# Mamba block between two feed-forward halves, one core: depthwise convolution of two of four channel blocks on TensorE, output projection added by VectorE from its bank, and a segment's side work placed anew

## Chip, cores and metric

One core of a Trainium2 chip. The metric is the device time of one launch in microseconds, the median over several runs. The launch gets all inputs in HBM and writes one output there.

## The reference, cut to what matters

The input has 4 sequences of 1024 tokens with 256 channels, float32 throughout. Three sublayers follow one another: a gated feed-forward part (three cycles of a small coupling network), a selective state-space (Mamba) block, and the feed-forward part again. The change lies in the middle one:

```
xn   = rmsnorm(layernorm(x)) * norm_w             # 256 channels
skip = xn @ skip_w.T ;  x = xn @ in_w.T           # 512 channels
xc[t] = conv_b + sum_k x[t-3+k] * conv_w[:, k]    # depthwise, 4 taps
x    = silu(xc)
delta = softplus((x @ wd1.T) @ wd2.T + wd2_b) ;  B, C = x @ wB.T, x @ wC.T
h[t] = exp(delta[t] * A) * h[t-1] + (delta[t] * x[t]) * B[t]    # 512 x 16 states
y[t] = sum_n h[t, :, n] * C[t, n] + W_D * x[t]
out  = (y * silu(skip)) @ out_w.T ;  result = resid + out
```

## The kernel before, in words

`build` (L1459) runs three programs behind one another, with all engines meeting in between: `ffn` on the input, `mamba`, and `ffn` again with the output stored. Only `mamba` (L719), the last lines of `kernel` and nothing of the feed-forward parts are touched.

**Segments and units.** `mamba` cuts the tokens into 8 segments of 512 (two halves of each sequence). The 512 channels are 4 blocks of 128 partitions (c = 0 to 3). A segment i is 32 units: for each pair of blocks (q = 0, 1) and each of the 16 states n, one unit. K counts units over all segments. Each engine has its own program that walks over K; semaphores with counts tie them. In one unit:

- GpSimd (`drive`, L1155) multiplies dx by the broadcast row of B into u, 128x1024. It may be four units ahead (U_RING).
- ScalarE (`decay`, L957) writes exp(delta * A) of both blocks into one of two PSUM tiles a_bank. It may refill one when the unit two before is done with it. In even segments it also copies the last column of each scan to `carry` (L969), which the odd segments start from.
- VectorE (`scan`, L1285) runs the recurrence along the 512 tokens of both blocks, one operand in PSUM. In 20 of 32 units it also multiplies by the row of C (`weigh`, L1297). In the 12 others (POOL_N: 0, 2, 5, 7, 10, 12 of each 16) the scan goes to SBUF and GpSimd weighs it (L1167), three units later.
- TensorE (`add_up`, L1442) adds the weighed states into y_bank by a product with the identity. At units 2 and 18 `feed_through` (L1430) starts a new sum with the D term, after `finish` (L1307, VectorE, units 1 and 17) has taken the last one and multiplied it by the gate.
- SyncE loads the rows of B and C, two units to a transfer, into rings of three.

**Side work.** Beside the recurrence of segment i, segment i + 1 is prepared (p = i + 1): input projection ("in", L1405), convolution, SiLU (L1027), projection to delta's rank, B and C ("xproj", L1410, copied by L1035 and stored to DRAM by SyncE at row pair 9), step size ("dt", L1414, copied by L1040), softplus (L1047), dx = delta * x on GpSimd (L1176). The skip projection of segment i itself gives the gate (tanh on ScalarE, L1112; `gate_skip` on VectorE, L1347), the output projection of segment i - 1 ("out", L1419) is copied by ScalarE (`take_out`, L1117) and added to x_tok by GpSimd (`out_add`, L1184), and the tokens of segment i + 2 are normalised (L979) and turned ("turn", L1399; L1001).

Two tables written by hand set the order: `PLACES` gives the units at which TensorE does each piece, `AT` the units at which the other engines do theirs. An engine does its side work of a unit behind that unit's recurrence. All TensorE side work goes through two banks, w_bank, in turn; `released` says whose signal frees a use for the next but one. Segment 0 is prepared ahead of the recurrence, in the a_banks.

**Convolution.** ScalarE's `accumulate` (L1019) starts an accumulator (it shares dx's storage) with the last tap and the bias. `convolve` (L1337) on VectorE adds the three other taps from the bank, shifted by one to three tokens, three scalar_tensor_tensor in place, each waiting for the one before. Since the second half of a sequence needs the last three tokens of the first, `keep_spill` (L1314, L1319, L1323) computes their part in three small operations per block when a first half is prepared, and `accumulate` puts it in by three single-column operations (L1017).

**Norms.** `norms(1, 0)` and `norms(1, 1)`, at units 5 and 10 of segment 0, compute the scales of the later tokens in operations of 128x16 (L1216 to L1230).

Of the kernel before, what the change touches and what calls it, by code (L numbers as in the profile page):

```python
# [718 lines left out]
def mamba(nc, mem, bc_rows):  # L719
# [21 lines left out]

    PLACES = {
        "in": ((0, 0), (1, 1), (3, 3), (4, 4)),
        "out": ((6, 6), (7, 7)),
        "xproj": ((10, 10),),
        "skip": ((11, 11), (14, 14), (19, 19), (20, 20)),
        "dt": ((13,), (15,), (16,), (17,)),
        "turn": ((24,), (25,)),
# [19 lines left out]
        "dx": (23, 24),  # L768
        "out_add": (13, 14),
# [27 lines left out]
    def exists(i, kind):  # L797
        return {"out": puts_out(i), "skip": core(i), "turn": turns(i)}.get(kind, prep(i))
# [22 lines left out]

    def released(use):

        i, kind, c = use
        p = i + 1
        if use[:2] == (-1, "in"):
            return "spill", c + 1
        return {"turn": ("xn", 2 * p + c + 3), "out": ("out_there", 2 * (i - 1) + c + 1), "in": ("conv", KE * p + c + 1),
                "xproj": ("proj", p + 1), "dt": ("step", KE * p + c + 1), "skip": ("gated", KE * i + c + 1)}[kind]

    with ExitStack() as ctx:
# [34 lines left out]
        one_col = sb("one_col", [P, 1])  # L866

# [8 lines left out]
            "xn_tok", "xn", "z", "work_done", "acc", "taps", "spill_part", "spill", "conv", "x",  # L876
            "proj", "bc_stored", "tanh_s", "gated", "step", "delta", "dx0", "dx1",
            "brow0", "brow1", "brow2", "crow0", "crow1", "crow2",
            "u", "a", "scan", "carry", "hc", "hc_pool", "y_dve", "y_pool", "y", "out_there", "out_added")}
# [16 lines left out]
        def _(sp):  # L896
            for i in range(-1, SEGS):
                for r in range(PASS):
# [17 lines left out]
                    if prep(i) and r == 9:  # L916
# [4 lines left out]
        def _(act):  # L921
# [83 lines left out]
            def accumulate(i, c):  # L1005
# [4 lines left out]
                if c == 0 and i > 0:  # L1010
                    act.wait_ge(S["u"], i * UNITS)
                lo = 0
                if ph == 1:
                    lo = TAPS - 1
                    act.wait_ge(S["spill"], p // 2 * KE + c + 1)
# [7 lines left out]
            def silu(i, c):  # L1023

                p = i + 1
                act.wait_ge(S["conv"], p * KE + c + 1)
# [494 lines left out]
```

## Time and profile before

| | us |
|---|---|
| median of 3 runs (lowest to highest) | 1326.85 (1325.11 to 1328.06) |
| the profiled execution, its own time | 1325.21 |
| its span in the trace | 1323.4 |
| VectorE busy | 1184.1 (89%) |
| TensorE busy | 1061.0 (80%) |
| GpSimd busy | 872.6 (66%) |
| ScalarE busy | 774.8 (59%) |
| recurrence of `mamba` (first scan to last weighing) | 224.8 to 1131 |

Busy is the share of the span in which an engine has an instruction under way. Matmuls are pipelined and their ends modelled, so TensorE's share is not its share at peak; a float32 product stands as two instructions. Rows of the timeline merge neighbouring instructions of one kind; within a row they overlap a little, so the distance between starts is what one costs. "[x <-E]" is idle time of the engine ahead of the instruction and what ended it. DVE is VectorE, ACT ScalarE, POOL GpSimd, PE TensorE.

### The profile page before, as it was taken

The page shows a single profiled execution, that of the slowest core. Times are in us where ns is not written, and L with a number is a line of the kernel's source. Part 1 is how long each engine was busy: PE and PEld are TensorE (multiplying, and loading weights), DVE is VectorE, ACT ScalarE, POOL GpSimd, SP SyncE. Part 2 cuts the span into 40 slices and gives each one's busy share as a digit, 9 for nine tenths or more (in the row PEclk, how much of TensorE's full clock was granted, in tenths as well). Part 3 has the DMA queues.
Part 4 walks back from the last instruction along what each step waited for, and adds up shares of the span by engine and source line. Part 5 has one row for each costly group of instructions (what it writes and reads, how often), then busy time and mean ns, then how long its engine had stood idle before and what let it go on. Part 6 is the DMA issues. An engine that isn't in the chain of part 4 may idle for free. (4 is left out here: it accounts for less than half of the span.)

```text
span 1323.4 us, 10922 instructions
## 1 busy us (share of the span) xinstructions
PE 1061.0 (80%) x2688; PEld 456.6 (35%) x2688; DVE 1184.1 (89%) x1768; ACT 774.8 (59%) x1321; POOL 872.6 (66%) x390
## 2 busy tenths in 40 slices
PE   3999746687889788888878988987897867799973
PEld 2434212233343343334334333432432422444421
DVE  3765898999999999999999999999999999576587
ACT  2656658757456566745666664665674434265665
POOL 0000004889989999998999999899999999000000
PEclk9999978799999999999989989999998889899998
DMA  6000003244543535343444444445444443000003
GB/s 207 1 1 1 1 1 113 96 160 133 170 141 130 181 112 185 127 159 128 149 169 141 165 142 149 140 126 191 139 149 162 137 177 112 0 1 1 1 1 128
DMA packets 48000, 146.56 MB, mean 111 GB/s; under 512 B 5504, under 2 KB 14336, under 8 KB 47936
## 3 DMA queue, kind: packets, MB, share of 16 engines
q1 hardware_dynamic: 47440, 145.03, 33.1%
q10 hardware_dynamic: 496, 0.82, 0.2%
q8 instruction: 22, 0.36, 0.1%
q14 instruction: 42, 0.34, 0.1%
HBM read 141.05 MB, written 4.72 MB: 110 GB/s over the span
## 5 line engine op out<-in xcount | busy, mean ns | idle before, releaser
L1155 POOL TENSOR_TENSOR late<-m_dx,m_brow 128x1024 f32<-128x1024 f32 x256 | 597.7, 2363 | 6.7 <-DVE m_a_bank L1285 6.5
L957 ACT ACTIVATE m_a_bank<-m_delta,m_negA 128x512 f32<-128x512 f32 x512 | 335.1, 683 | 174.6 <-DVE m_hc L1297 134.0
L1442 PE MATMUL m_y_bank<-m_hc,ident 128*128 128x512 f32 x640 | 332.4, 645 | 116.1 <-DVE m_hc L1297 115.4
L1167 POOL TENSOR_TENSOR m_hc_pool<-m_hid,m_crow 128x1024 f32<-128x1024 f32 x96 | 226.8, 2363 | 31.0 <-DVE m_hid L1285 30.6
L1442 PEld LDWEIGHTS m_y_bank<-m_hc,ident 128*128 128x128 f32 x640 | 119.6, 201 | 305.1 <-DVE m_hc L1297 186.7
L1297 DVE TENSOR_TENSOR m_hc<-m_a_bank,m_crow 128x512 f32<-128x512 f32 x320 | 203.0, 677 | 0.0
L1285 DVE TENSOR_TENSOR_SCAN m_a_bank<-m_a_bank,m_carry,late 128x512 f32<-128x512 f32 x160 | 196.4, 1274 | 1.1 <-ACT m_a_bank L957 0.8
L1285 DVE TENSOR_TENSOR_SCAN m_a_bank<-m_a_bank,late 128x512 f32<-128x512 f32 x160 | 186.7, 1212 | 7.0 <-ACT m_a_bank L957 3.7
L1442 PE MATMUL m_y_bank<-m_hc_pool,ident 128*128 128x512 f32 x384 | 188.0, 613 | 4.9 <-POOL m_hc_pool L1167 4.9
L1176 POOL TENSOR_TENSOR m_dx<-m_delta,m_x 128x1024 f32<-128x1024 f32 x16 | 38.0, 2377 | 216.5 <-ACT m_delta L1047 216.5
L1285 DVE TENSOR_TENSOR_SCAN m_hid<-m_a_bank,m_carry,late 128x512 f32<-128x512 f32 x96 | 117.7, 1269 | 0.0
L1405 PE MATMUL m_w_bank<-m_xn,w 128*128 128x512 f32 x240 | 112.5, 596 | 2.5 <-DVE m_dx L1337 2.4
L1285 DVE TENSOR_TENSOR_SCAN m_hid<-m_a_bank,late 128x512 f32<-128x512 f32 x96 | 111.8, 1206 | 1.4 <-ACT m_a_bank L957 1.4
L1442 PEld LDWEIGHTS m_y_bank<-m_hc_pool,ident 128*128 128x128 f32 x384 | 75.7, 199 | 104.1 <-issue 88.6
L432 PE MATMUL f_pair<-f_h,w 128*128 128x512 f32 x192 | 92.5, 609 | 8.4 <-ACT f_h L549 8.4
L969 ACT ACTIVATE m_carry<-m_a_bank 128x2 f32<-128x2 f32 x80 | 13.5, 169 | 111.1 <-DVE m_hc L1297 111.1
L1430 PE MATMUL m_y_bank<-m_x,m_diag_d 128*128 128x512 f32 x64 | 41.2, 778 | 33.8 <-DVE m_gate L1307 33.8
L1419 PE MATMUL m_w_bank<-w,m_gate 128*128 128x256 f32 x256 | 59.1, 384 | 9.6 <-DVE m_dx L1337 8.1
L1405 PEld LDWEIGHTS m_w_bank<-m_xn,w 128*128 128x128 f32 x240 | 44.9, 190 | 62.9 <-issue 53.8
L481 PE MATMUL f_pair<-f_z,w 128*128 128x512 f32 x128 | 65.4, 592 | 0.0
L549 ACT ACTIVATE f_h<-f_a,w 128x512 f32<-128x512 f32 x96 | 63.6, 712 | 1.0 <-DVE f_a L271 1.0
L1337 DVE SCALAR_TENSOR_TENSOR m_dx<-m_w_bank,m_conv,m_dx 128x511 f32<-128x511 f32 (+2 forms) x84 | 62.2, 741 | 1.1
(148 smaller groups left out, 1237.9 us busy)
## 6 DMA issues: line engine op xcount, KB each, us to landing
m_brow<-bc_rows SPq DMA_DIRECT2D x128, 512.0 KB, 5.0
m_crow<-bc_rows SPq DMA_DIRECT2D x128, 512.0 KB, 4.1
x_tok<-x_in SPq DMA_DIRECT2D x4, 1024.0 KB, 8.6
out<-x_tok SPq DMA_DIRECT2D x3, 1024.0 KB, 4.8
w<-w_in SPq DMA_DIRECT2D x1, 1024.0 KB, 11.6
out<-x_tok SPq DMA_DIRECT2D x4, 256.0 KB, 2.1
w<-w_in SPq DMA_DIRECT2D x1, 750.0 KB, 10.4
w<-w_in ACTq DMA_DIRECT2D x1, 512.0 KB, 6.0
```

The costliest lines, as they stand in the source:

```text
L432: last = nc.tensor.matmul(pair[2][:, h, :], w(w256, W256, "w2", k), h1[:, k, half(h)], start=k == 0, stop=k == KD - 1)
L481: last = nc.tensor.matmul(out[:, m, :], second, z[:, b % 2, 1, half(n)], start=False, stop=True)
L549: nc.scalar.activation(h1[:, m, half(h)], source, ACT.Gelu, bias=w128[:, o:o + 1]).then_inc(h1_ready, 1)
L957: nc.scalar.activation(a_bank[K % 2][:, j, :], delta[:, i % 2, c, :], ACT.Exp, scale=negA[:, c, n:n + 1]).then_inc(S["a"], 1)
L1155: nc.gpsimd.tensor_tensor(u[:, K % U_RING, :, :], dx[:, i % 2, 2 * q:2 * q + 2, :], brow[:, K // 2 % ROW_RING, K % 2, :].unsqueeze(1).to_b ...
L1167: nc.gpsimd.tensor_tensor(hc_pool[:, before % POOL_RING, :, :], hid[:, before % POOL_RING, :, :], crow[:, K // 2 % ROW_RING, K % 2, :].uns ...
L1285: nc.vector.tensor_tensor_scan(hid[:, pool_before(K) % POOL_RING, j, :] if by_pool(K) else a, a, u[:, K % U_RING, j, :], 0.0 if i % 2 == 0 ...
L1297: nc.vector.tensor_tensor(hc[:, before % HC_RING, j, :], a_bank[K % 2][:, j, :], crow[:, K // 2 % ROW_RING, K % 2, :], ALU.mult).then_inc( ...
L1337: nc.vector.scalar_tensor_tensor(a[:, s:], b[:, 0:BANK - s], conv[:, c, k:k + 1], a[:, s:], ALU.mult, ALU.add)\
L1405: op = nc.tensor.matmul(b, w256[:, part, o:o + P], xn[:, (p if kind == "in" else i) % 2, part, :], start=part == 0, stop=part == KD - 1)
L1419: op = nc.tensor.matmul(b[:, part * DIM:(part + 1) * DIM], gate[:, d, at:at + P], col("out", d, DIM), start=d == 0, stop=d == KE - 1)
L1442: op = nc.tensor.matmul(y_bank[:, j, :], ident[:, :], source[:, before % ring, j, :], start=False, stop=K % PASS == PASS - 1)
```

## The change

Blocks 2 and 3 (PE_CONV) are convolved by TensorE in all segments but segment 0's preparation: ScalarE copies the projection to `raw` in SBUF behind its last three tokens, TensorE multiplies four shifted windows of it by four diagonal matrices (`diag_w`) and sums them in a bank ("taps"), and the SiLU reads that bank with the bias. No spill is kept for these blocks. Blocks 0 and 1 stay as they were. VectorE adds the output projection straight from its bank; ScalarE's copy and GpSimd's add are gone. The two tables are new. The four tensor_tensor of `norms` (L1218, L1220, L1227, L1230) become scalar_tensor_tensor with a factor 1. The final statistics are taken inside VectorE's loop, which is longer. The scratch for descriptors is given as 8192.

```diff
+    PE_CONV = (2, 3)
     PLACES = {
         "in": ((0, 0), (1, 1), (3, 3), (4, 4)),
         "out": ((6, 6), (7, 7)),
-        "xproj": ((10, 10),),
-        "skip": ((11, 11), (14, 14), (19, 19), (20, 20)),
-        "dt": ((13,), (15,), (16,), (17,)),
-        "turn": ((24,), (25,)),
+        "skip": ((9, 9), (10, 10), (24, 24), (25, 25)),
+        "taps": ((), (), (12, 12, 13, 13), (13, 13, 14, 14)),
+        "xproj": ((18, 18),),
+        "dt": ((20,), (21,), (22,), (23,)),
+        "turn": ((27,), (28,)),
     }
     AT = {
         "acc": (2, 3, 5, 6),
-        "silu": (8, 8, 8, 8),
-        "out_there": (9, 10),
-        "proj": (12,),
-        "tanh_s": (13, 16, 21, 22),
-        "step": (15, 17, 18, 19),
-        "softplus": (20,),
-        "xn_tok": (23, 24),
-        "xn": (26, 27),
-        "z": (28, 29),
-        "conv": (2, 3, 5, 6),
-        "gate": (13, 16, 21, 22),
+        "tanh_s": (11, 12, 26, 27),
+        "silu": (17, 17, 17, 17),
+        "proj": (20,),
+        "step": (22, 23, 24, 25),
+        "softplus": (25,),
+        "xn_tok": (25, 26),
+        "xn": (29, 30),
+        "z": (30, 31),
+        "conv": (2, 3),
+        "out_add": (8, 9),
+        "gate": (11, 12, 26, 27),
         "finish": (1, 17),
-        "dx": (23, 24),
-        "out_add": (13, 14),
+        "dx": (28, 29),
     }
...
+        if kind == "in" and p > 0 and c in PE_CONV:
+            return "raw", 2 * p + c - 1
...
+        raw = sb("raw", [P, 2, TAPS - 1 + BANK])
+        diag_w = sb("diag_w", [P, 2, TAPS, P])
...
-                    if prep(i) and r == 9:
+                    if prep(i) and r == (13 if i >= 0 else 9):
                         sp.wait_ge(S["proj"], i + 2)
...
+                if c in PE_CONV and p > 0:
+
+                    if ph == 0:
+                        act.wait_ge(S["none"], 1)
+                    nc.scalar.activation(raw[:, c - 2, 0:TAPS - 1], none[:, :] if ph == 0 else raw[:, c - 2, BANK:],
+                                         ACT.Copy).then_inc(S["history"], 1)
+                    act.wait_ge(S["history"], 2 * (p - 1) + c - 1)
+                    nc.scalar.activation(raw[:, c - 2, TAPS - 1:], b, ACT.Copy).then_inc(S["raw"], 1)
+                    return
+                if c in PE_CONV:
+                    nc.scalar.activation(raw[:, c - 2, BANK:], b[:, BANK - TAPS + 1:], ACT.Copy).then_inc(S["raw"], 1)
...
-                act.wait_ge(S["conv"], p * KE + c + 1)
+                if c in PE_CONV and p > 0:
+                    nc.scalar.activation(x[:, p % 2, c, :], work_there((i, "taps", c)), ACT.Silu,
+                                         bias=conv[:, c, TAPS:TAPS + 1]).then_inc(S["x"], 1)
+                    return
+                act.wait_ge(S["conv"], conv_count(p, c))
...
-                if c == 0:
-                    act.wait_ge(S["out_added"], 2 * i)
-                if c >= 2:
+                if i > 0 or c >= 2:
                     act.wait_ge(S["gated"], i * KE + c - 1)
...
-                    nc.vector.tensor_tensor(square, rstd[:, ts], rstd[:, ts], ALU.mult).then_inc(S["square"], 1)
+                    nc.vector.scalar_tensor_tensor(square, rstd[:, ts], 1.0, rstd[:, ts], ALU.mult, ALU.mult)\
+                        .then_inc(S["square"], 1)
...
+            nc.vector.memset(none[:, :], 0.0).then_inc(S["none"], 1)
+            for c in PE_CONV:
+                for s in range(TAPS):
+                    op = nc.vector.tensor_scalar(diag_w[:, c - 2, s, :], ident[:, :], w512[:, c, o + s:o + s + 1], None,
+                                                 ALU.mult)
+            op.then_inc(S["diag_w"], 1)
...
+            def out_add(i, c):
+
+                dve.wait_ge(S["work_done"], USES.index((i, "out", c)) + 1)
+                dve.wait_ge(S["z"], 2 * i)
+                at = (i - 1) * HT + 2 * c
+                to = x_tok[:, at:at + 2, :].rearrange("p a d -> p (a d)")
+                nc.vector.tensor_tensor(to, to, bank_of((i, "out", c)), ALU.add).then_inc(S["out_added"], 1)
...
-            for K in range(-UNITS, TOTAL + 2):
+            for K in range(-UNITS, TOTAL + UNITS):
...
+                if K == TOTAL + 2:
+                    final_measure()
+                for c in due(k, "out_add") if puts_out(i) else ():
+                    out_add(i, c)
...
                 if K == AT["conv"][-1] - UNITS:
-                    for c in range(KE):
+                    for c in PE_CONV:
+                        convolve(i, c)
+                    for c in range(KE - len(PE_CONV)):
                         keep_spill(-1, c, 1)
                         keep_spill(-1, c, 2)
...
+                elif kind == "taps":
+                    if part == 0:
+                        pe.wait_ge(S["diag_w"], 1)
+                        pe.wait_ge(S["raw"], 2 * p + c - 1)
+                    op = nc.tensor.matmul(b, diag_w[:, c - 2, part, :], raw[:, c - 2, part:part + BANK],
+                                          start=part == 0, stop=part == TAPS - 1)
...
-    nc = bacc.Bacc("TRN2", target_bir_lowering=False, num_devices=1)
+    nc = bacc.Bacc("TRN2", target_bir_lowering=False, num_devices=1, dynamic_dma_scratch_size=8192)
```

## Rows read from the trace of the kernel before

**Rows 1.** Busy time by stretch: segments 0, 1, 2; columns named in the first row.
```profile
core 0: us, PE busy (x) PEld busy (x) DVE busy (x) ACT busy (x) POOL busy (x), PEclk, DMA share, GB/s
224.80:344.40 119.60, 87.31 (x176) 34.39 (x176) 117.52 (x131) 79.17 (x153) 107.15 (x48) 0.87 0.42 135
344.40:459.00 114.60, 95.28 (x225) 41.15 (x224) 114.19 (x138) 66.28 (x103) 109.42 (x50) 0.97 0.46 148
459.00:570.70 111.70, 96.07 (x225) 41.62 (x224) 109.15 (x125) 72.73 (x144) 108.51 (x49) 0.95 0.43 151
```
**Rows 2.** Groups of instructions, VectorE, segment 2; busy, mean ns, idle before, releasers.
```profile
L1285 DVE TENSOR_TENSOR_SCAN m_a_bank<-m_a_bank,late 128x512 f32<-128x512 f32 x40 | 46.7, 1212 | 1.9 <-POOL late L1155 1.0 <-ACT m_a_bank L957 0.9
```
**Rows 3.** Timeline, GpSimd, segment 0; start, length, instruction.
```profile
241.40 7.00 POOL L1155 TENSOR_TENSOR late<-m_dx,m_brow 128x1024 f32<-128x1024 f32 x3
```
**Rows 4.** Timeline, VectorE, a convolution in segments 2 (even) and 1 (odd).
```profile
470.30 2.34 DVE L1285 TENSOR_TENSOR_SCAN m_a_bank<-m_a_bank,late 128x512 f32<-128x512 f32 x2
472.55 1.27 DVE L1297 TENSOR_TENSOR m_hc<-m_a_bank,m_crow 128x512 f32<-128x512 f32 x2
473.73 2.31 DVE L1337 SCALAR_TENSOR_TENSOR m_dx<-m_w_bank,m_conv,m_dx 128x511 f32<-128x511 f32 x3
...
353.91 0.73 DVE L1337 SCALAR_TENSOR_TENSOR m_dx<-m_w_bank,m_conv,m_dx 128x511 f32<-128x511 f32 x1
356.44 2.46 DVE L1285 TENSOR_TENSOR_SCAN m_a_bank<-m_a_bank,m_carry,late 128x512 f32<-128x512 f32 x2
```
**Rows 5.** Waits of segment 7 (first row), then timeline of the tail.
```profile
DVE m_gate L1347 <- ACT m_th L1112: 2.9, 1, 2.9
...
1141.57 0.60 ACT L1117 ACTIVATE m_th<-m_w_bank 128x512 f32<-128x512 f32 x1 [2.86 <-PE m_w_bank L1419]
1142.24 1.26 POOL L1184 TENSOR_TENSOR x_tok<-x_tok,m_th 128x512 f32<-128x512 f32 x1 [2.19 <-ACT m_th L1117]
```
**Rows 6.** TensorE, segments 2 and 3: projection, restarts behind finish; then one stretch's clock.
```profile
502.26 3.60 PE L1410 MATMUL m_w_bank<-m_x,w 128*96 128x512 f32 x8
...
525.92 3.26 PE L1430 MATMUL m_y_bank<-m_x,m_diag_d 128*128 128x512 f32 x4 [1.92 <-DVE m_gate L1307]
...
531.15 1.88 PE L1442 MATMUL m_y_bank<-m_hc_pool,ident 128*128 128x512 f32 x4
...
640.50 1.98 PE L1430 MATMUL m_y_bank<-m_x,m_diag_d 128*128 128x512 f32 x4 [2.29 <-DVE m_gate L1307]
...
526.00:530.00 4.00, 4.00 (x6) 1.70 (x7) 4.00 (x4) 2.62 (x6) 4.00 (x3) 0.57 0.65 260
```
**Rows 7.** Timeline, ScalarE, around the four SiLUs of segment 2.
```profile
488.97 1.28 ACT L1027 ACT_TABLE_LOAD   x1
...
493.92 1.30 ACT L957 ACTIVATE m_a_bank<-m_delta,m_negA 128x512 f32<-128x512 f32 x2
```
**Rows 8.** Timeline around the softplus, segments 2 (first three) and 3.
```profile
526.21 0.67 ACT L1040 ACTIVATE m_delta<-m_w_bank,w 128x512 f32<-128x512 f32 x1
...
535.30 2.34 DVE L1285 TENSOR_TENSOR_SCAN m_hid<-m_a_bank,late 128x512 f32<-128x512 f32 x2 [0.35 <-ACT m_a_bank L957]
...
540.24 1.08 ACT L979 ACTIVATE m_tmp_u<-x_tok,m_shift_n,m_scale_n 128x256 f32<-128x256 f32 x2
...
648.17 1.30 ACT L957 ACTIVATE m_a_bank<-m_delta,m_negA 128x512 f32<-128x512 f32 x2
649.81 2.46 DVE L1285 TENSOR_TENSOR_SCAN m_hid<-m_a_bank,m_carry,late 128x512 f32<-128x512 f32 x2
```
**Rows 9.** Timeline, VectorE, norms in segment 0.
```profile
248.68 4.35 DVE L1218 TENSOR_TENSOR m_roots<-m_rstd 128x16 f32<-128x16 f32 x1
...
271.59 2.28 DVE L1225 SCALAR_TENSOR_TENSOR m_shift<-moments,m_rstd 128x16 f32<-128x16 f32 x1
```
**Rows 10.** Timeline, VectorE, prologue ahead of the first scan.
```profile
202.32 0.75 DVE L1337 SCALAR_TENSOR_TENSOR m_dx<-m_a_bank,m_conv,m_dx 128x511 f32<-128x511 f32 x1 [2.77 <-ACT m_dx L1019]
...
213.32 0.27 DVE L1314 TENSOR_SCALAR m_spill<-m_a_bank,m_conv 128x3 f32<-128x3 f32 x1
...
214.02 0.34 DVE L1248 SCALAR_TENSOR_TENSOR x_tok<-late,coef,x_tok 128x128 f32<-128x128 f32 x1
```

More of the change, by code:

```diff
@@ L797, in exists @@
     def exists(i, kind):
-        return {"out": puts_out(i), "skip": core(i), "turn": turns(i)}.get(kind, prep(i))
+        return {"out": puts_out(i), "skip": core(i), "turn": turns(i), "taps": prep(i) and i >= 0}.get(kind, prep(i))
     def bank_name(i, kind, c, index):
@@ L825, in released @@
         p = i + 1
-        if use[:2] == (-1, "in"):
+        if kind == "in" and p == 0 and c not in PE_CONV:
             return "spill", c + 1
-        return {"turn": ("xn", 2 * p + c + 3), "out": ("out_there", 2 * (i - 1) + c + 1), "in": ("conv", KE * p + c + 1),
+        if kind == "in" and p > 0 and c in PE_CONV:
+            return "raw", 2 * p + c - 1
+        return {"turn": ("xn", 2 * p + c + 3), "out": ("out_added", 2 * (i - 1) + c + 1), "in": ("conv", conv_count(p, c)),
+                "taps": ("x", KE * p + c + 1),
                 "xproj": ("proj", p + 1), "dt": ("step", KE * p + c + 1), "skip": ("gated", KE * i + c + 1)}[kind]
@@ L875, in mamba @@
             "negA", "expA", "late_by_dve", "late_straight", "late_added", "late_stats", "moments", "root", "square", "rstd", "diag_d", "final_stats", "constants",
-            "xn_tok", "xn", "z", "work_done", "acc", "taps", "spill_part", "spill", "conv", "x",
+            "xn_tok", "xn", "z", "work_done", "acc", "history", "raw", "none", "diag_w", "taps", "spill_part", "spill", "conv", "x",
             "proj", "bc_stored", "tanh_s", "gated", "step", "delta", "dx0", "dx1",
             "brow0", "brow1", "brow2", "crow0", "crow1", "crow2",
-            "u", "a", "scan", "carry", "hc", "hc_pool", "y_dve", "y_pool", "y", "out_there", "out_added")}
+            "u", "a", "scan", "carry", "hc", "hc_pool", "y_dve", "y_pool", "y", "out_added")}
         block = ctx.enter_context(nc.Block())
@@ L1014, in accumulate @@
                     lo = TAPS - 1
-                    act.wait_ge(S["spill"], p // 2 * KE + c + 1)
+                    act.wait_ge(S["spill"], p // 2 * 2 + c + 1)
                     for j in range(lo):
@@ L1341, in convolve, with final_measure @@
                         keep_spill(i, c, s)
+            def out_add(i, c):
[4 more added lines that the diff above has]
+                nc.vector.tensor_tensor(to, to, bank_of((i, "out", c)), ALU.add).then_inc(S["out_added"], 1)
+            def final_measure():
+                dve.wait_ge(S["out_added"], 2 * 2 * HALVES)
+                for t in range(2 * BT):
+                    op = nc.vector.bn_stats(final_stats[:, t, :], x_tok[:, t, :])
+                op.then_inc(S["final_stats"], 1)
+                dve.wait_ge(S["final_stats"], 1)
+                for t in range(2 * BT):
+                    nc.vector.bn_aggr(moments[:, t, :], final_stats[:, t, :])
             def gate_skip(i, c):
-                if c == 0 and puts_out(i):
-                    dve.wait_ge(S["out_there"], 2 * i)
                 dve.wait_ge(S["tanh_s"], i * KE + c + 1)
```

40 lines of the change are left out of this document (12 added, 28 removed).

## The prediction

> **What bounds the kernel now.** I cut the span into its parts with the table of busy time by stretch [rows 1]: the recurrence runs from 224.8 to 1131 us, 68% of the span, as eight segments of 32 units. Apart from the prologue ahead of it and the hand-over behind it, all the work that the change touches lies there. VectorE (DVE) is busy 109.15 of the 111.70 us of segment 2 and 114.19 of the 114.60 of segment 1, so it sets the pace. Odd segments start from carries and keep the convolution's spill, and are longer. The groups of instructions give what little DVE waits: in segment 2, 1.0 us for POOL and 0.9 for ScalarE (ACT) before scans [rows 2], the rest in gaps of 0.3 to 0.4. GpSimd (POOL) is close behind: three products in a row take 7.00 us, one every 2.32 [rows 3]. A segment has 32 products for u, 12 weighings and 2 for dx, 46 x 2.32 = 106.7 us, and POOL's two output adds on top (108.5 to 109.4 busy). So DVE work that goes is worth its full time only down to some 107 us a segment, and only if what is moved makes no new wait. TensorE (PE) has 96 of 112 us busy, with modelled ends.
>
> **The change, part by part.**
>
> *Convolution.* On DVE the three operations of a block stand with 2.31 us in an even segment, 2.25 of it their own (neighbours overlap, as the scan pair of 2.34 shows, behind which the next starts after 2.25); with the spill in an odd segment it is 2.53, 353.91 to 356.44 [rows 4]. Two blocks go from each of seven segments: 4.5 or 5.1 us.
>
> *Output adds.* DVE gets two adds of 128x512 with one operand in PSUM. The nearest row has the same engine, operation and kinds of operand: two in 1.18 us (472.55 to 473.73), 0.59 each [rows 4]. I take 1.2 us a segment (segments 1 to 7); bounds 1.1 and, at the price of a convolution's operation, 2.31 / 3, 1.5. POOL loses 2.5 us, ACT two copies of 0.60 [rows 5].
>
> *PE.* Eight products for the taps. The four products (8 instructions) of the projection take 3.6 us [rows 6], so 7 us a segment, bounded by 14 at half clock. PE is not the bound on average, 96 + 7 of 109; where it could be is a rival below.
>
> *ACT on blocks 2 and 3.* Copies replace scaled copies of like size, and three single-column operations each go in even segments; the SiLU reads a bank instead of an accumulator. I price it at nothing: units 2 to 6 of these segments are where DVE convolves and ACT is ahead. Bounds minus 0.5 and plus 0.5.
>
> *SiLUs at unit 17.* At unit 8 today the table load starts at 488.97 and the next decay only at 493.92 [rows 7]: 5 us, which two scans and a weighing on DVE just cover. At 17 the next unit is a POOL one (no weighing on DVE, 1.2 us less cover), set off by finish (1.2 us more), but the decay of 17 is itself released later by a carry: counting the rows through from the start of scan 16, the decay of 18 is ready at 7.45 us and DVE at 2.25 + 3.43 + 1.19 = 6.87. Late by 0.6 in even segments; without the carry copies and with longer scans, nothing in odd ones.
>
> *Projection at 18 and 20.* It now stands behind finish(17) and PE's feed-through. Today PE goes from the feed-through to its third group in 5.23 us in segment 2 (525.92 to 531.15); in segment 3, where the feed-through takes 1.98 and not 3.26, it is some 3.5 [rows 6]. With 3.6 for the projection, 0.6 for ACT's copy and 0.95 for the carry and half a decay, scan 21's input stands 17.4 us after scan 16's start at the slow rate, 15.8 at the fast; DVE wants it at 16.6. Late by 0 to 0.9; 0.5 in even segments, 0 in odd ones.
>
> *Softplus at 25, beside step(3) and the first xn_tok.* Units 24, 25, 26 have the pattern of 19, 20, 21. Today scan 21 waits 0.35 us [rows 8]. Two things are added ahead of the next decay: the step of 0.67, done a unit earlier today, and the xn_tok pair of 1.08. So 0.35 + 0.67 + 1.08 = 2.1 us late at scan 26 in even segments. In odd ones that decay has 0.9 us in hand (its first half is over at 648.86, the scan starts at 649.81 [rows 8]), so 0.85. One more xn_tok and a tanh at 26 put scan 27 0.25 late in even ones.
>
> *Sum of new waits:* 0.6 + 0.5 + 2.1 + 0.25 = 3.45 us in an even segment, 0.9 to 1.0 in an odd one. They replace 2.55 and 0.4.
>
> *POOL.* Its dx products move to 28 and 29. It gets to u(28) only when scan 24 has ended, and the softplus is over before scan 25 ends, so it loses at most the time of one product; a wait for scan 26 ahead of weighing 26 comes to it, from its lead. With 106.7 us of work in segments of 109 to 111.5 it keeps a lead, and the 1.0 us DVE waits for it goes.
>
> *SP.* The store of B and C moves from row pair 9 to 13, behind the row loads that wait for unit 21, so the projection (by then copied) never holds the queue. One issue stands ahead of the next row load either way: nothing.
>
> *Norms* (four tensor_tensor become scalar_tensor_tensor). In segment 0 the tensor_tensor of 128x16 takes 4.35 us and the scalar_tensor_tensor of 128x16 takes 2.28 [rows 9], for 16 elements a partition. Both forms wait, so I give the edit 0; its bounds are minus 4.2 and plus 2.3.
> The Trainium skill says of this (SBUF — State Buffer, on the shared port pair) that VectorE and GpSimd lock one pair of ports for a whole instruction, and that a VectorE instruction with two SBUF inputs needs it; by that rule, with which the trace agrees, the new form gains nothing, and by a rule that tied the stall to tensor_tensor the sum would be 4.2 lower. It also speaks for the new output add, one of whose inputs is in PSUM.
>
> *Prologue.* The spill of two blocks goes from DVE's unbroken run to the first scan: 0.70 each (213.32 to 214.02), minus 1.4 [rows 10]. The eight scaled identities of 128x128, at most the 0.34 us of the 128x128 operation at 214.02, are 2.7 us in the 2.77 that DVE idles ahead of the first convolution [rows 10]: nothing; uncovered they would cost 2.7.
>
> *Last segment and tail.* DVE's wait of 2.9 us for the gate, held up by the output copies and POOL's adds, goes [rows 5]; 1.2 of adds come and a POOL wait of 0.3 goes: minus 2.0, of which I take 1.7. After the recurrence ACT's copy (0.60) and POOL's add (1.26) give way to one DVE add of 0.68 [rows 5]: minus 1.2. The loop's longer range and the move of the final statistics cost nothing: they run while PE multiplies.
>
> *Sum.* Prologue -1.4. Segment 0: -4.5, old waits of 2.1 (119.60 less 117.52) for new ones of 3.45, -3.1. Segments 2, 4, 6: -4.5 + 1.2 - 2.55 + 3.45 = -2.4 each, -7.2. Segments 1, 3, 5: -5.1 + 1.2 - 0.4 + 1.0 = -3.3 each, -9.9. Last segment -1.7, tail -1.2. In all -24.5 us. The profiled execution took 1325.21 us (span 1323.4), which gives 1300.7; the median of the runs shown, 1326.85, stands 1.6 higher, so 1302.3.
>
> **Rivals.**
>
> *The new waits don't come; POOL is the limit.* For it: DVE's own work is then 105.8 (even) and 110.4 (odd), and half a unit of ACT's lead would swallow the 0.6 and 0.5. Against it: today's 0.35 us at the softplus shows ACT with no reserve there. Even segments would fall to 106.7 (-5.0), odd ones by 4.3, segment 0 by 6.6: -1.4 - 6.6 - 15 - 12.9 - 3.2 = -39, 1288.
>
> *The clock at PE's restart.* In segment 2 the groups behind finish run mostly at the lower of the two levels, 1.2 GHz (granted clock 0.57 from 526 to 530), after PE has idled 1.92 us [rows 6]. If the projection too runs there it takes 7.2 in place of 3.6, and finish, feed-through, projection, copy and decay become one chain through four engines: 3.6 later, of which DVE feels some 2 to 3.4 in each of seven segments. Against it: odd segments restart at 2.4 GHz, and PE idles less with the taps. -24 + 7 x 2 = -10, 1316; at worst 1326.
>
> *PE becomes the bound ahead of finish (slower).* From the end of unit 4 to finish(17) PE has 13 sums of 1.72 (half the projection's eight instructions, less their overlap), the outputs' 6.9, two skips and the taps, 3.4 + 6.9: 39.6 us. DVE reaches finish(17) after 41.1 in an even segment (five POOL units of 2.25, eight of its own at 2.25 + 1.18, two adds and two gates at 0.6), 42.4 in an odd. A microsecond at 1.2 GHz costs half a microsecond; with over 10 us of it in that stretch in each of seven segments, DVE would wait 3.5 us at each finish and all the gain would be gone. At 15 us it waits some 5.5: +39 - 24, 1342. Against it: PE has no gap there after which the clock fell.
>
> *It doesn't do what it says:* DVE's busy time falls, but the old waits, moved, take all of it: 1327.
>
> **Numbers.** Forecast with its neighbourhood (1293 to 1309) 0.58; POOL limit 0.12; restart chain 0.19, a few hundredths of it within 0.2%; PE bound 0.06; no gain 0.05. Range 1291 to 1316: most of the POOL case and the restart case at 2 us a segment. A measurement here can tell 0.2% (2.7 us) from no change. Faster 0.87, same 0.06, slower 0.07.
>
> **What would show it.** DVE's STT on convolution banks down from 12 to 6 a segment; busy 105.9 (even) and 110.4 (odd); segments of 109.3 and 111.4; a wait of about 2 us for ACT at scan 26 (0.9 odd), under 1 at 18 and 21; POOL without idle cost to DVE; norms' stalls still 2 to 4 us; first scan at 223.4. Wrong if waits at finish(17) exceed 1 us (PE), if scan 21 waits over 2 us (restart), or if scan 26 starts on time (POOL limit).

## The result, and the profile after

The changed kernel takes 1316.5 us, the median of 4 runs (1315.76 to 1318.55), against 1326.42 of 4 runs of the kernel before: a ratio of 0.9927, with a 95% interval of 0.991 to 0.9944. It is faster, as forecast, but by 9.9 us and not by 24.5. The profiled execution took 1316.35 us with a span of 1314.6 (before: 1325.21 and 1323.4). Of the twelve executions of e5 below, one took 1823.45 us at a granted clock of 0.557 and is left out of what is said of e5.

First the busy time by engine, from the page of the changed kernel, and then its table of busy time by stretch for segments 1, 2, 5 and 6 (columns as in [rows 1]).

```profile
PE 1090.7 (83%) x2800; PEld 479.5 (36%) x2800; DVE 1162.0 (88%) x1727; ACT 760.6 (58%) x1298; POOL 853.1 (65%) x374
```
```profile
341.80:456.40 114.60, 98.85 (x242) 43.91 (x240) 110.50 (x127) 64.93 (x103) 107.25 (x47) 0.99 0.44 147
456.40:568.00 111.60, 100.35 (x241) 44.56 (x240) 106.11 (x121) 70.18 (x138) 106.05 (x47) 0.97 0.47 151
...
794.00:909.80 115.80, 101.58 (x241) 44.98 (x240) 110.53 (x128) 65.08 (x103) 107.24 (x47) 0.96 0.43 146
909.80:1018.60 108.80, 97.51 (x233) 43.20 (x232) 105.89 (x122) 64.73 (x126) 104.31 (x46) 0.98 0.46 153
```

Beside [rows 1] the reader is to see that VectorE's work fell as worked out: 114.19 to 110.50 in segment 1 (110.4 was forecast), 109.15 to 106.11 in segment 2 (105.9 was forecast). But segments 1 and 2 are as long as before, 114.6 and 111.6. The eight segments' lengths, from first scan to first scan and to the last weighing for segment 7, are 117.9, 114.6, 111.6, 114.4, 111.6, 115.8, 108.8 and 105.1 us; before, 119.7, 114.6, 111.7, 114.6, 111.8, 114.6, 111.7 and 107.4. The forecast had 21.9 us less in them, and 6.3 came. Segments 1, 3 and 5 fall short by 3.3, 3.1 and 4.5, segments 2 and 4 by 2.3 and 2.2, segment 0 by 1.3; segments 6 and 7 beat it by about half a microsecond each.

The work that went was replaced by waits. The groups of instructions on VectorE in segment 2 (as [rows 2]):

```profile
L1303 DVE TENSOR_TENSOR_SCAN m_a_bank<-m_a_bank,late 128x512 f32<-128x512 f32 x40 | 46.6, 1212 | 1.2 <-ACT m_a_bank L970 1.2
L1303 DVE TENSOR_TENSOR_SCAN m_hid<-m_a_bank,late 128x512 f32<-128x512 f32 x24 | 28.0, 1208 | 4.1 <-ACT m_a_bank L970 4.1
...
L1355 DVE SCALAR_TENSOR_TENSOR m_dx<-m_w_bank,m_conv,m_dx 128x511 f32<-128x511 f32 (+2 forms) x6 | 4.5, 743 | 0.1
...
L1367 DVE TENSOR_TENSOR x_tok<-x_tok,m_w_bank 128x512 f32<-128x512 f32 x2 | 1.4, 680 | 0.0
```

The six operations of convolution and the two new adds stand there as planned, and the wait for GpSimd is gone. In its place are 5.3 us of waits for ScalarE's decay; before, it was 1.3 us for ScalarE and 1.0 for GpSimd. By unit, the waits before scans are: in segments 2 and 4, 0.64 at scan 18, 0.66 at 21, 1.24 at 24, 2.8 at 26; in segments 1 and 3, 0.77 and 0.59 at 21, 0.91 at 24, 2.35 at 26; in segment 5, 1.93 at 21 and the rest alike. Segment 6 has no wait at 21, 0.3 at 24 and 1.82 at 26. The forecast had 0.6, 0.5, nothing and 2.1 in an even segment, and 0.85 at scan 26 alone in an odd one. So scan 18 is right, scan 24 was not foreseen, scan 26 is 0.7 over in even segments and 1.5 in odd ones, and the 0.25 forecast at scan 27 did not come.

What ScalarE waited for stands in the table of waits over the recurrence (total us, number of waits, longest):

```profile
ACT m_proj L1063 <- PE m_w_bank L1448: 32.9, 7, 7.0
...
ACT m_delta L1068 <- PE m_w_bank L1452: 25.9, 15, 2.8
...
DVE m_hid L1303 <- ACT m_a_bank L970: 23.9, 15, 2.8
```

ScalarE waits for the projection (seven times, once for each segment that is prepared) and then for the products of the step size. The chain in segment 3, first TensorE's timeline, then ScalarE's, then VectorE's (scans 21, 24 and 26):

```profile
633.51 3.50 PE L1468 MATMUL m_y_bank<-m_x,m_diag_d 128*128 128x512 f32 x4 [3.85 <-DVE m_gate L1325]
636.84 1.88 PE L1480 MATMUL m_y_bank<-m_hc,ident 128*128 128x512 f32 x4
638.56 3.60 PE L1448 MATMUL m_w_bank<-m_x,w 128*96 128x512 f32 x8
...
645.52 1.12 PE L1452 MATMUL m_w_bank<-m_proj,w 64*128 64x512 f32 x2
...
654.03 1.12 PE L1452 MATMUL m_w_bank<-m_proj,w 64*128 64x512 f32 x2
```
```profile
642.19 0.59 ACT L1063 ACTIVATE m_proj<-m_w_bank 96x512 f32<-96x512 f32 x1 [5.64 <-PE m_w_bank L1448]
...
651.36 0.69 ACT L1068 ACTIVATE m_delta<-m_w_bank,w 128x512 f32<-128x512 f32 x1 [2.80 <-PE m_w_bank L1452]
...
655.19 0.69 ACT L1068 ACTIVATE m_delta<-m_w_bank,w 128x512 f32<-128x512 f32 x1 [0.15 <-PE m_w_bank L1452]
655.89 1.28 ACT L1075 ACT_TABLE_LOAD   x1
```
```profile
643.50 2.46 DVE L1303 TENSOR_TENSOR_SCAN m_hid<-m_a_bank,m_carry,late 128x512 f32<-128x512 f32 x2 [0.59 <-ACT m_a_bank L970]
...
652.76 2.47 DVE L1303 TENSOR_TENSOR_SCAN m_a_bank<-m_a_bank,m_carry,late 128x512 f32<-128x512 f32 x2 [0.91 <-ACT m_a_bank L970]
...
662.31 2.46 DVE L1303 TENSOR_TENSOR_SCAN m_hid<-m_a_bank,m_carry,late 128x512 f32<-128x512 f32 x2 [2.35 <-ACT m_a_bank L970]
```

TensorE stands for 3.85 us at the feed-through until finish(17) is done, and only then does the projection behind it, though its last input was there at 630.7 (the end of the SiLUs). From 633.51 to the last product of the step size at 654.03 it has no idle row. Each product comes late, ScalarE stands before the step of each (2.80 at the worst, and with it the decay for scan 24), and the last step, still held by TensorE (0.15), puts the start of the softplus, the table load at 655.89, 3.1 us after the start of scan 24. Scan 26 pays for it.

The recorded expectations below weigh two theories. **Theory A**: TensorE is late, because it idles for finish, restarts at the lower level of its clock, and only then does the projection. **Theory B**: ScalarE has more work between units 17 and 27 than fits, whoever feeds it. Theory A has two halves, which e7 and e8 part. *The place*: the projection is queued behind the wait for finish. *The clock*: what is queued there restarts at the lower level.

### The profile page after: what moved, and what is told of

Read it like the earlier page. It is cut to its first block and busy times, and to the rows that moved or that the text cites. A ratio compares the mean times of both kernels' runs of the same rounds, so it can differ in the third digit from the quotient of the medians.

```text
span 1314.6 us, 11061 instructions
## 1 busy us (share of the span) xinstructions
PE 1090.7 (83%) x2800; PEld 479.5 (36%) x2800; DVE 1162.0 (88%) x1727; ACT 760.6 (58%) x1298; POOL 853.1 (65%) x374
## 5 line engine op out<-in xcount | busy, mean ns | idle before, releaser
L1480 PE MATMUL m_y_bank<-m_hc,ident 128*128 128x512 f32 x640 | 326.1, 634 | 85.8 <-DVE m_hc L1315 85.8
L1480 PE MATMUL m_y_bank<-m_hc_pool,ident 128*128 128x512 f32 x384 | 183.6, 601 | 0.0
L1303 DVE TENSOR_TENSOR_SCAN m_hid<-m_a_bank,late 128x512 f32<-128x512 f32 x96 | 111.8, 1206 | 13.6 <-ACT m_a_bank L970 13.5
L256 DVE TENSOR_SCALAR f_cpl<-f_cpl,f_slope,f_base 128x512 f32<-128x512 f32 x32 | 17.4, 543 | 42.2 <-ACT f_cpl L581 42.1
```

The source lines that it names most:

```text
L1303: nc.vector.tensor_tensor_scan(hid[:, pool_before(K) % POOL_RING, j, :] if by_pool(K) else a, a, u[:, K % U_RING, j, :], 0.0 if i % 2 == 0 ...
L1480: op = nc.tensor.matmul(y_bank[:, j, :], ident[:, :], source[:, before % ring, j, :], start=False, stop=K % PASS == PASS - 1)
```

## The experiments

Each was run beside the kernel before, on the same chip as it: 1327.5 us (7 runs) for the first four, 1327.39 (17 runs) on another chip for the others. Each edit is against the changed kernel, where nothing else is said, and "..." marks lines left out. A caution for small differences of totals: the feed-forward part behind `mamba`, which no edit touches, takes 179.3 us in the profiled executions of the changed kernel and of e8 (granted clock 0.956), 179.9 in the kernel before, and 180.8 to 181.5 in the others (0.94). So the readings below go by segment.

**The projection one unit earlier, ahead of finish (e1).**

```diff
-        "xproj": ((18, 18),),
+        "xproj": ((17, 17),),
```

> The changed kernel with one number changed: the projection to rank, B and C at TensorE's unit 17 in place of 18, so that it stands ahead of the feed-through that waits for finish(17), and no longer behind it. Theory A (TensorE gets late: it idles 2.4 to 3.9 us for finish(17), restarts at the low clock, and only then does the projection, so that scans 21 and 24 and in part 26 wait for ScalarE, which waits for TensorE): the waits at scan 21 (0.6 to 1.9 us) and 24 (0.9 to 1.2) go, scan 26 waits 0.9 (odd) or 2.1 (even) in place of 2.35 and 2.8; sum over the segments some 15 us, 1301 us. Theory B (ScalarE itself has more work between units 17 and 27 than fits, whoever feeds it): the waits only change places, 1316 us. A third outcome, the feed-through late by 1.5 us making sums and finish late: slower than 1316.

Measured: 1297.68 us (1297.12 to 1298.28), ratio 0.9776 (0.9761 to 0.979). One unit in a table takes 19 us off. Its busy time by stretch for segments 1 and 2, and its timelines of TensorE and of ScalarE in segment 3:

```profile
340.70:451.90 111.20, 99.25 (x241) 44.02 (x240) 110.33 (x128) 65.34 (x103) 106.65 (x47) 0.98 0.45 151
451.90:560.50 108.60, 99.01 (x241) 44.10 (x240) 105.87 (x121) 70.42 (x138) 106.42 (x47) 0.98 0.45 155
```
```profile
622.56 3.67 PE L1448 MATMUL m_w_bank<-m_x,w 128*96 128x512 f32 x8 [0.53 <-ACT m_x L1051]
626.07 1.88 PE L1468 MATMUL m_y_bank<-m_x,m_diag_d 128*128 128x512 f32 x4
...
631.78 1.98 PE L1480 MATMUL m_y_bank<-m_hc,ident 128*128 128x512 f32 x4 [0.40 <-DVE m_hc L1315]
...
635.33 1.98 PE L1480 MATMUL m_y_bank<-m_hc,ident 128*128 128x512 f32 x4 [0.51 <-DVE m_hc L1315]
```
```profile
644.30 0.69 ACT L1068 ACTIVATE m_delta<-m_w_bank,w 128x512 f32<-128x512 f32 x1
645.01 1.28 ACT L1075 ACT_TABLE_LOAD   x1
```

The 3.67 us of the projection now lie in the time in which TensorE stood for finish. It comes to the feed-through without a gap and at full speed (four instructions in 1.88), and soon waits for VectorE again (0.40, 0.51): it has caught up. The last step does not wait for TensorE, and the softplus starts 1.55 us after scan 24 (643.46 to 645.01), not 3.1. VectorE's waits in this run are 0.64 at scan 18 and 1.95 at scan 26 in even segments, 0.8 at scan 26 in odd ones, and none at 21 or 24. These are the forecast's own 0.6, 2.1 and 0.85, and the segments of 111.2 and 108.6 stand beside its 111.4 and 109.3. Theory B is out: the waits at 21 and 24 went, they did not change places. Both halves of theory A allow this, since the idle stretch and the place went together: the seven restarts behind finish(17) in segments 0 to 6 are all at the full clock here (granted 1.00).

**The first two xn_tok out of the softplus's stretch (e2), and both edits (e3).**

```diff
-        "xn_tok": (25, 26),
+        "xn_tok": (21, 22),
```

> The changed kernel with the two xn_tok pieces (ScalarE, 1.08 us each) at units 21 and 22 in place of 25 and 26. Theory A: ScalarE idles 1.0 to 2.8 us for dt products ahead of the steps of units 22 and 23, so the pieces cost nothing there, and the wait at scan 26 falls by the 1.08 us of the first in segments 0 to 5: minus 6.5 us, 1310. Theory B (ScalarE is full from 17 to 27): moving work within the stretch changes nothing, 1316.

> Both edits. Theory A: the gains add, as long as xn_tok at 21 and 22 still finds ScalarE free or ahead: scan 26 waits 0 (odd) to 1.0 (even); 1295 us. If with the earlier projection ScalarE has no idle time at 22 and 23 any more, xn_tok there delays scan 23 or 24 and the sum is some 1299. Theory B: 1316.

Measured for e2: 1310.88 us, ratio 0.9877 (0.9862 to 0.9891). The wait at scan 26 falls from 2.35 to 1.37 in odd segments and from 2.8 to 1.82 in segments 0, 2 and 4, by 0.98 each: the term "xn_tok pair of 1.08" of the forecast, paid nearly in full. Segment 6 stays at 1.82. The other waits moved too, though the edit touches nothing of TensorE: segments 1 and 2 restarted TensorE at the full clock and lost their waits at 21 (and 0.9 us at 24), segments 3 to 6 restarted at the lower one (scan 21 waits 2.1 in segment 3). Over the eight segments these changes nearly cancel, which is luck, so that the total can be set beside the expectation of 1310. Measured for e3: 1293.19 us (1291.87 to 1297.76), ratio 0.975 (0.9728 to 0.9772). The two gains add up (19 and 6 against 23). Odd segments then have no wait at all and take 110.3 us, even ones 107.5 with 0.65 at scan 18 and 0.96 at scan 26 left. For that last wait the timeline shows ScalarE at work without an idle row from 529.91 to scan 26's decay at 537.60 in segment 2: the last step, the softplus of 2.0 us between two table loads of 1.28, carry and decay. What is left is ScalarE's own work.

**The new order with all four blocks convolved by VectorE (e4).** No taps, no copies to `raw`; the spill and its counts for four blocks again.

```diff
-    PE_CONV = (2, 3)
+    PE_CONV = ()
...
-        "taps": ((), (), (12, 12, 13, 13), (13, 13, 14, 14)),
+        "taps": ((), (), (), ()),
...
-        "conv": (2, 3),
+        "conv": (2, 3, 5, 6),
...
```

> The changed kernel with its new order of side work and the output add on VectorE, but with all four blocks convolved by VectorE as before (no TensorE taps, spill for all blocks). If VectorE's time in the first units is worth its full length and the later waits are local hand-overs: plus 4.5 us in segments 0, 2, 4, 6, plus 5.1 in 1, 3, 5, plus 1.4 in the prologue, 34.7 in all, 1351 us, so the new order alone would be slower than before by 24. If the taps on TensorE are what makes it late and sets up the waits at 21 to 26, these waits shrink here and the time is nearer 1335.

Measured: 1356.91 us, ratio 1.0222 (1.0207 to 1.0238). Its segments 1 and 2 by stretch:

```profile
351.00:471.30 120.30, 97.29 (x225) 41.94 (x224) 115.50 (x140) 64.89 (x101) 107.29 (x47) 0.94 0.42 140
471.30:587.30 116.00, 95.34 (x225) 40.78 (x224) 110.35 (x127) 71.48 (x142) 106.15 (x47) 0.97 0.42 146
```

Without the move of the convolution the new order is 29 us slower than the kernel before. VectorE's work rises by 5.0 us in segment 1 and 4.2 in segment 2, the size of the terms 5.1 and 4.5. The waits before scans of segment 2 are those of the changed kernel to about 0.1 us (0.54, 0.78, 1.24, 2.81), so neither taps nor copies make them: the order does. In this order the convolution on TensorE is worth 40 us (1356.9 less 1316.5), where 35 was expected, 33 of it from the work of seven segments. The excess lies where this execution restarted TensorE at a lower clock than the changed kernel: segment 0 (6.8 us longer; granted clock 0.50 and not 1.00, scan 21 waits 2.01), segment 1 (5.7) and segment 6 (6.4; 0.51 and not 1.00). Segment 5 lost 3.9 only, less than its work. Another 2.2 us is the untouched feed-forward part.

**The output add on VectorE alone, in the old order (e5).** The kernel before with ScalarE's copy and GpSimd's add taken out, VectorE's two adds at units 8 and 9 and the final statistics inside its loop. The edit is against the kernel before.

```diff
-        "out_there": (9, 10),
...
-        "out_add": (13, 14),
+        "out_add": (8, 9),
...
```

> The kernel before with one part of the change alone: VectorE adds the output projection from its bank at units 8 and 9; ScalarE's copies and GpSimd's adds go, the gate no longer waits for them; tables, convolution and norms as before. By my sum: plus 1.2 us in each of segments 1 to 7 (8.4), minus the 1.0 us VectorE waits for GpSimd in segments 2, 4 and 6, minus the 0.86 us at scan 13 there if the output copies made it, minus 3.2 in segment 7, minus 1.2 in the tail: about plus 1, 1328 us, within 0.2% of no change. A rival, that the add costs more from a bank than the weighing it was priced by: over 1331.

Measured: 1330.19 us, the median of eleven executions (1326.45 to 1331.75), ratio 1.0016 (1.0007 to 1.0026). The adds alone bring nothing; about 1328 was expected. Segments 2, 4 and 6 take 111.5 us, 0.3 less: VectorE's idle time fell from 2.5 to 1.1 (the wait for GpSimd went, the one at scan 13 shrank to 0.26) and 1.2 of work came (109.2 to 110.4). Odd ones take 116.8, 2.2 longer: half of that is the work that came (114.2 to 115.3), half is this wait at scan 13 in VectorE's timeline, where 0.26 stood before:

```profile
398.72 2.47 DVE L1264 TENSOR_TENSOR_SCAN m_a_bank<-m_a_bank,m_carry,late 128x512 f32<-128x512 f32 x2 [1.35 <-ACT m_a_bank L956]
```

**The step size a unit earlier, on top of e3 (e6).**

```diff
-        "dt": ((20,), (21,), (22,), (23,)),
+        "dt": ((19,), (20,), (21,), (22,)),
...
-        "proj": (20,),
-        "step": (22, 23, 24, 25),
+        "proj": (19,),
+        "step": (21, 22, 23, 24),
```

> Both edits that gave 1293 us, and the step-size products, their steps and the projection's copy one unit earlier (dt 19 to 22, step 21 to 24, proj 19), so that no step stands at unit 25 ahead of the softplus. By the theory the wait at scan 26 (0.96 us in even segments, 0 in odd ones) falls by the 0.67 us of that step: minus 2.7 us, 1290. If the copy at 19 comes before the projection is done, scan 20 waits instead and nothing is gained: 1293.

Measured: 1292.93 us (1291.57 to 1294.17), ratio 0.9742 (0.973 to 0.9755), the same as e3. This missed: the wait at scan 26 fell by 0.33 in segments 2, 4 and 6 (0.96 to 0.63) and not by the length of a step, and segment 0 gained a wait of 0.64 at scan 24. In segment 2 ScalarE now stands 0.90 us before the third step, until TensorE has its product (529.88), and from there works without an idle row up to scan 26's decay. Why only half of the step's length was won was not tried.

**Filler ahead of finish, the projection left behind it (e7).** Half of the projection's products are computed at unit 17 and thrown away; the whole projection follows at 18 as in the changed kernel. So TensorE idles less before the restart, but the place stays.

```diff
-        "xproj": ((18, 18),),
+        "xproj": ((17, 18, 18),),
...
-                    for d in (2 * part, 2 * part + 1):
+                    for d in ((0, 1), (0, 1), (2, 3))[part]:
...
```

> The changed kernel (projection at 18) with two products of the projection done once more at unit 17, ahead of the feed-through, as filler (the result is the same; TensorE does 4 instructions more a segment). It leaves the projection's place behind finish(17) as it is, and shortens TensorE's idle time ahead of it, so that the clock may stay at 2.4 GHz. If the low clock at the restart has a share in the waits: feed-through in 2.0 us in place of 2.4 to 3.5, and the waits at 21 to 26 some 1 us shorter a segment, 1309 us. If the place alone does it: 1316.

Measured: 1312.77 us (1308.76 to 1314.27), ratio 0.9887 (0.9874 to 0.9901). First the clock of the restart in segment 3 (granted clock in the column before the last two), which in the changed kernel had been this:

```profile
633.50:637.00 3.50, 3.49 (x5) 1.67 (x6) 3.50 (x4) 2.43 (x4) 3.37 (x2) 0.56 0.79 279
```

With the filler it is this, followed by the rows of TensorE and of ScalarE:

```profile
635.50:639.00 3.50, 3.47 (x8) 1.60 (x9) 3.50 (x4) 2.46 (x4) 3.38 (x2) 1.00 0.74 297
```
```profile
635.53 1.99 PE L1468 MATMUL m_y_bank<-m_x,m_diag_d 128*128 128x512 f32 x4 [1.36 <-DVE m_gate L1325]
```
```profile
655.70 0.69 ACT L1068 ACTIVATE m_delta<-m_w_bank,w 128x512 f32<-128x512 f32 x1
656.40 1.28 ACT L1075 ACT_TABLE_LOAD   x1
```

The granted clock is 1.00 (2.4 GHz) in place of 0.56 (about 1.2), the feed-through takes 1.99 and not 3.50. The waits at scans 21 and 24 are gone in odd segments (0.3 left at 24 in even ones), and segments 1 to 5 take 112.9 and 109.9. But scan 26 still waits 2.35 and 2.8, since the softplus still starts 3.1 us after scan 24 (653.27 to 656.40). So both halves of theory A count, and the steps can be read segment by segment: from the changed kernel to e7, without the low clock, -1.7, -1.7, -1.5, -1.7, -2.9 and 0 in segments 1 to 6, 9.5 us; from e7 to e1, with the place mended, -1.7, -1.3, -1.8, -1.3, -1.7 and -1.3, 9.1 us. Segment 6 fits: the changed kernel restarted there at the full clock by itself, and the filler brought it nothing. In segment 0 e7 loses 4.7, mostly by longer stalls of the norms (8.21, 2.35 and 2.38 us; 0.98, 2.27 and 5.82 in the changed kernel), which with 1.6 us of the untouched part is why its time does not show the 9.5.

**The norms back to tensor_tensor (e8).**

```diff
-                    nc.vector.scalar_tensor_tensor(square, rstd[:, ts], 1.0, rstd[:, ts], ALU.mult, ALU.mult)\
+                    nc.vector.tensor_tensor(square, rstd[:, ts], rstd[:, ts], ALU.mult)\
```

(and the three others alike)

> The changed kernel with the four operations of norms put back to tensor_tensor. In the changed kernel the scalar_tensor_tensor of 16 elements take 0.98, 2.27 and 5.82 us where they meet GpSimd, 8.5 us too long in all, as much as before. So both forms wait for GpSimd, and the edit is worth nothing: 1316 us, within 2 us (how many GpSimd instructions one meets is a matter of where it falls). The rival, that the new form waits less: slower than 1318.

Measured: 1315.57 us (1313.68 to 1318.07), ratio 0.9914 (0.9901 to 0.9927), the changed kernel's within the interval. So the edit is worth nothing that shows. The total alone does not prove it, since two things cancel in the profiled execution: its eight small operations take 13.6 us (10.0 in the changed kernel), and segments 2 and 4 are 1.7 us shorter each by the clock, as shown below. But e7, with the new form, has 13.9, and the kernel before, with the old one, 9.9. The stall falls on other operations of the norms from kernel to kernel, in either form. VectorE and GpSimd in segment 0, of the changed kernel:

```profile
263.82 5.82 DVE L1235 SCALAR_TENSOR_TENSOR m_shift<-moments,m_rstd 128x16 f32<-128x16 f32 x1
...
264.96 2.35 POOL L1186 TENSOR_TENSOR m_hc_pool<-m_hid,m_crow 128x1024 f32<-128x1024 f32 x1
267.27 2.34 POOL L1174 TENSOR_TENSOR late<-m_dx,m_brow 128x1024 f32<-128x1024 f32 x1
```

and of e8:

```profile
246.96 7.88 DVE L1226 TENSOR_TENSOR m_roots<-m_rstd 128x16 f32<-128x16 f32 x1
...
252.46 2.35 POOL L1174 TENSOR_TENSOR late<-m_dx,m_brow 128x1024 f32<-128x1024 f32 x1
257.46 2.34 POOL L1174 TENSOR_TENSOR late<-m_dx,m_brow 128x1024 f32<-128x1024 f32 x1 [2.65 <-DVE m_a_bank L1303]
```

Each stall ends where a GpSimd instruction ends and GpSimd has no next one ready: 269.64 against 267.27 + 2.34 = 269.61, and 254.84 against 252.46 + 2.35 = 254.81. The short ones end at an instruction's end too (272.44 against 272.41 in e8), with GpSimd going on at once.

The e8 run also shows the clock by itself. In segment 2 the order of work is the same as in the changed kernel and so is the idle time ahead of the restart, 2.37 us. The changed kernel:

```profile
519.12 2.41 PE L1468 MATMUL m_y_bank<-m_x,m_diag_d 128*128 128x512 f32 x4 [2.37 <-DVE m_gate L1325]
521.32 3.19 PE L1480 MATMUL m_y_bank<-m_hc,ident 128*128 128x512 f32 x4
524.35 3.60 PE L1448 MATMUL m_w_bank<-m_x,w 128*96 128x512 f32 x8
```

and e8:

```profile
524.13 1.98 PE L1468 MATMUL m_y_bank<-m_x,m_diag_d 128*128 128x512 f32 x4 [2.37 <-DVE m_gate L1325]
525.96 1.88 PE L1480 MATMUL m_y_bank<-m_hc,ident 128*128 128x512 f32 x4
527.67 3.60 PE L1448 MATMUL m_w_bank<-m_x,w 128*96 128x512 f32 x8
```

From the restart to the projection it is 5.23 us in one (granted clock 0.67) and 3.54 in the other (1.00), 1.69 apart, and the segments are 111.6 and 109.9, 1.7 apart. The 1.69 goes through to VectorE whole.

## Why the prediction was right and wrong

- **Convolution and output adds: right.** VectorE's busy time is within 0.3 us of the forecast in segments 1 and 2. The adds cost 1.4 (two of 680 ns) by their durations, and 1.1 to 1.2 by e5, against 1.2. E4 gives the convolution's price in VectorE's work as 5.0 and 4.2, against 5.1 and 4.5.
- **GpSimd's wait gone, and GpSimd not the bound: right.** VectorE has no wait for it in segment 2. Without most other waits (e3, e6) even segments come down to 107.4, near the 106.7 named for that rival, but what is left there is still ScalarE, 1.3 to 1.6 us.
- **SiLUs at unit 17: right**, 0.64 at scan 18 against 0.6, and none in odd segments.
- **"Projection at 18 and 20": this is the step that failed.** It was priced as one event, scan 21's input, "late by 0 to 0.9", and as that it was nearly right for even segments (0.66 against 0.5) and low for odd ones (0.59, 0.77 and 1.93 against 0). What it missed is that the chain does not end there. TensorE had over 20 us of work without a gap queued behind the restart, so the delay was carried on to each product of the step size, to ScalarE's steps (a wait at scan 24 of 0.91 and 1.24, forecast nowhere), and to the softplus. In segment 1 this is the whole shortfall of 3.3: 0.77 at scan 21, 0.91 at scan 24 and 1.5 more than forecast at scan 26. With the projection one unit earlier (e1) all three are gone.
- **"Softplus at 25": right by its own arithmetic, wrong in what it started from.** It took scan 24's neighbourhood to be on time. With the projection in time (e1) its 2.1 and 0.85 are measured as 1.95 and 0.8; with it late, 2.8 and 2.35. One of its terms was tried singly and holds: the xn_tok pair of 1.08 is worth 0.98 (e2). The step's 0.67 was worth 0.33 (e6).
- **PE at nothing on average: too coarse.** "96 + 7 of 109" was on the high side (98.9 and 100.4 us busy), and the rival ahead of finish did not come: finish(17) waits 0.47 us in segment 0 and nothing in the others. But TensorE did not idle less with the taps, as was argued: ahead of the feed-through it was 1.92 us in even and 2.29 in odd segments, and is 2.37 and 3.86 now. The taps end at unit 14, and the step-size products that stood at units 15 to 17 had gone behind finish(17); that this is the cause was not tried alone. And a resource with spare time in a segment had none in the 20 us behind its own wait, which is where the change put the urgent work.
- **The restart rival: nearest to what came, and its 1316 in part luck.** Its mechanism was the projection at half clock, 7.2 us. The projection ran in 3.60, at full clock, in segments 1 to 5. The low clock fell on the feed-through and the sum behind it. It accounts for about 9.5 of the 18.5 us that e1 takes back in segments 1 to 6, and the place for the rest. Its test ("scan 21 waits over 2 us") would have refused it; the longest was 1.93. What was said against it, "odd segments restart at 2.4 GHz", was read from segment 3 alone [rows 6]. The same trace has segments 1 and 5 at the lower level (granted clock 0.56 and 0.64), and segment 6, an even one, at full:

```profile
414.20 3.48 PE L1430 MATMUL m_y_bank<-m_x,m_diag_d 128*128 128x512 f32 x4 [2.29 <-DVE m_gate L1307]
```

- **Norms: right** that the edit is worth nothing that shows: the stalls are 8.6 us too long in all in the changed kernel (0.98 + 2.27 + 5.82 less 3 x 0.17), 8.4 before (4.35 + 2.28 and one of 2.32). But the stall's size was taken as 2 to 4 us, and e8 and e7 have 7.88 and 8.21 in one.
- **Prologue: nearly right.** The first scan starts at 223.92, 0.9 earlier and not 1.4. But all of `mamba` started 0.34 us later (188.87 against 188.53), behind a part that the change does not touch, so its own share is 1.2. The eight scaled identities were hidden. The convolution took 9.2 against 9.0, which is the rest.
- **Last segment and tail: right.** 2.3 us less in segment 7 (1.7 forecast), whose wait of 2.9 [rows 5] is gone; 1.2 less from the last scan to the end of `mamba` (13.8 to 12.6). These rows of VectorE's timeline take the place of ScalarE's copy and GpSimd's add:

```profile
1133.57 0.65 DVE L1367 TENSOR_TENSOR x_tok<-x_tok,m_w_bank 128x512 f32<-128x512 f32 x1
1134.55 0.69 DVE L1367 TENSOR_TENSOR x_tok<-x_tok,m_w_bank 128x512 f32<-128x512 f32 x1 [0.33 <-PE m_w_bank L1457]
```

- **Segment 0: 1.3 us over.** Its work fell by 4.2 and not 4.5, and its idle time rose to 4.5 and not 3.45: 2.8 at scan 26, 0.86 at scan 24 (not foreseen) and 0.47 at finish.

Open: why e5's odd segments get their longer wait at scan 13, and why the step a unit earlier brought half of its length (e6). Neither was tried alone.

## What to carry to other kernels

When work with a deadline moves on an engine that executes in order, ask first what that engine will be waiting for just ahead of it: here the same projection cost nothing that shows one unit earlier, inside TensorE's wait for finish, and 19 us behind that wait, about half by its place and half by the low clock after the idle stretch. Price a late input down to the last piece that hangs on it, not to the first consumer; a queue without a gap carries the delay on until it next runs dry. Take a term's start as a condition: the softplus term was right only if what came before it was on time. And before a risk is put aside with one row, look at the same row in every segment.

## What the runs showed of the hardware

- **The same idle time led to both clock levels.** In segment 2 TensorE idled 2.37 us in both kernels shown above, and the feed-through and the sum took 2.41 + 3.19 us in one and 1.98 + 1.88 in the other. The changed kernel itself has both: after 2.37 us it restarted at full in segment 6 (1.98 + 1.88). After 3.86 us it restarted low in segment 1 (3.26), and e2 in the same segment at full (granted clock 1.00):

```profile
405.84 1.98 PE L1468 MATMUL m_y_bank<-m_x,m_diag_d 128*128 128x512 f32 x4 [3.86 <-DVE m_gate L1325]
```

  Of the 18 restarts behind finish(17) in segments 1 to 6 of the changed kernel, e2 and e8, all after 2.37 or 3.86 us idle, 12 came at the lower level (granted clock below 1.00 in the 3.5 us from the restart). In the changed kernel's segment 5 the idle time was that of segment 3 (3.86 and 3.85), and the low level lasted longer:

```profile
859.50 3.78 PE L1468 MATMUL m_y_bank<-m_x,m_diag_d 128*128 128x512 f32 x4 [3.86 <-DVE m_gate L1325]
863.07 2.98 PE L1480 MATMUL m_y_bank<-m_hc,ident 128*128 128x512 f32 x4
865.89 3.60 PE L1448 MATMUL m_w_bank<-m_x,w 128*96 128x512 f32 x8
```

  From restart to projection that is 6.39 us against 5.05 (633.51 to 638.56), 1.34 more; scan 21 waits 1.34 more (1.93 against 0.59), and the segment is 1.4 longer. With four throw-away instructions in the gap, which left 0.26 us of it in even and 1.36 in odd segments, none of the six restarts came at the lower level (e7). The Trainium skill (TensorE: Matmul & The Clock Gate, Part 1) says that the half rate is the default and that activity releases it. The traces agree that a restart can fall to it, and show besides that a kernel's schedule alone does not say which restarts will.
- **A small operation on VectorE can stand through several GpSimd instructions.** For 16 elements a partition, 0.17 us when free, it took up to 5.82 us in the changed kernel, 7.88 in e8 and 8.21 in e7. The Trainium skill (SBUF — State Buffer, SBUF: two separate sides) says that the shared pair of ports is locked for a whole instruction and that the other engine blocks meanwhile. The ends of the stalls agree with it. What the rows add is that the waiting operation did not get its turn at every end: in 7.88 us, more than three products of 2.32, GpSimd finished three instructions before the one at which the stall ended.
